# The second node stage of a three-layer graph network: the merge done head by head, with the bias inside it

## The reference

```
out = segment_sum(xl[src] * alpha, dst) + b1      # a softmax over the edges that end in a node, self loop included
h   = elu(out)                                    # what the second layer starts from
x   = layernorm(x + gatv2(h));  x = layernorm(x + gat(x))
```

## Time and profile before

| | us |
|---|---|
| median of 3 runs (4007.61 to 4011.79) | 4010.43 |
| profiled execution, its own time | 4004.83 |
| its span | 4003.0 |
| DVE busy in the span | 3296.9 (82%) |
| POOL busy in the span | 2765.2 (69%) |
| node stage 1: first L1360 to the MEMSET L1474 that opens edge stage 1 | 1319.49 to 1511.99 |

### The profile page before, as it was taken

One profiled execution on the slowest core, in us unless ns is written; L12 is line 12 of the kernel. 1 busy time (PEld: TensorE's weight loads), 2 busy tenths in 40 slices (PEclk: granted clock), 3 DMA queues, 4 the chain that ended last, 5 costly groups with the idle time before them and its releaser, 6 DMA issues. The chain is left out here.

```text
span 4003.0 us, 115501 instructions
## 1 busy us (share of the span) xinstructions
PE 3522.5 (88%) x30761; PEld 2584.0 (65%) x30762; DVE 3296.9 (82%) x10046; ACT 1278.9 (32%) x4356; POOL 2765.2 (69%) x3039
## 2 busy tenths in 40 slices
PE   6699999999999668999999999977678888787885
PEld 5577777777777456777777777745445555555543
DVE  6768888888888885888888888876688898888886
ACT  4433333333333463333333333324111111111113
POOL 5577777777776467777777777723777777777760
PEclk9899999999999899999999999989799999899989
DMA  4344444444443124444444444435455555555544
GB/s 99 116 131 136 136 131 136 136 135 132 134 136 106 58 70 135 136 135 131 136 136 135 131 136 136 131 96 186 134 143 140 143 145 143 141 144 138 144 109 129
DMA packets 279405, 520.84 MB, mean 130 GB/s; under 512 B 98391, under 2 KB 165121, under 8 KB 279313
## 3 DMA queue, kind: packets, MB, share of 16 engines
q0 software_dynamic: 120320, 338.39, 31.2%
q1 hardware_dynamic: 158993, 181.36, 15.1%
HBM read 484.05 MB, written 35.46 MB: 130 GB/s over the span
## 5 line engine op out<-in xcount | busy, mean ns | idle before, releaser
L704 POOL DMA_INDIRECT gathered<-table,idx x2496 | 2501.4, 1002 | 787.6 <-issue 526.0
L1120 PE MATMUL pS<-gathered,Dm 128*128 128x264 f32 x4992 | 1689.5, 422 | 107.7 <-DVE Dm L1533 58.9
L1520 DVE TENSOR_TENSOR acc_mem<-acc_mem,pS 128x264 f32 x2496 | 1043.6, 418 | 144.8 <-PE pS L1120 105.6
L1059 PE MATMUL pZ<-DT,x 128*128 128x128 bf16 x9984 | 1090.2, 221 | 14.1 <-DVE DT L1480 11.5
L1059 PEld LDWEIGHTS pZ<-DT,x 128*128 x9984 | 874.2, 98 | 325.0 <-issue 51.7
L873 ACT ACTIVATE reluT<-pZ 128x256 f32<-128x256 f32 x1664 | 637.1, 383 | 1128.5 <-PE pZ L1065 1098.6
L1120 PEld LDWEIGHTS pS<-gathered,Dm 128*128 128x128 f32 x4992 | 797.2, 200 | 239.5 <-DVE gathered L1551 104.9
L1065 PE MATMUL pZ<-ident,gathered 128*128 128x128 f32 x3328 | 934.6, 281 | 11.9 <-DMA gathered<-table,idx 11.8
L1551 DVE TENSOR_TENSOR gathered<-gathered 128x256 f32<-128x256 f32 x2496 | 941.6, 417 | 1.8 <-ACT gathered L865 1.0
L1533 DVE TENSOR_TENSOR Dm<-pS,rel_items 128x256 f32<-128x256 f32 x1239 | 513.8, 415 | 0.0
L1065 PEld LDWEIGHTS pZ<-ident,gathered 128*128 128x128 f32 x3328 | 470.4, 141 | 16.2 <-DMA gathered<-table,idx 14.3
(11 more groups left out here) (230 smaller groups left out, 3211.4 us busy)
## 6 DMA issues: line engine op xcount, KB each, us to landing
DT<-rel_dram SPq DMA_DIRECT2D x156, 512.0 KB
gathered<-table,idx POOLq DMA_INDIRECT x2496
table<-xls SPq DMA_DIRECT2D x147, 132.0 KB, 2.0
flags<-flag_dram SPq DMA_DIRECT2D x416, 32.0 KB
flags<-flag_dram SPq DMA_DIRECT2D x52, 256.0 KB
gathered<-table SPq DMA_DIRECT2D x98, 132.0 KB, 2.1
gathered<-in_x SPq DMA_DIRECT2D x98, 128.0 KB, 2.1
hx_dram<-gathered SPq DMA_DIRECT2D x49, 128.0 KB, 1.7
```

Of the source, the lines that this page charges most:

```text
L704: nc.gpsimd.indirect_dma_start(out=G[:, b, i, :], out_offset=None, in_=tab[l], in_offset=bass.IndirectOffsetOnAxis(ap=idx[:, b, i:i + 1], ...
L1059: mm = nc.tensor.matmul(z_slot(i)[:, half], x3[:, bass.ds(tk[i], 1), s, half].rearrange("p o c -> p (o c)"), moving, start=(s == 0), stop= ...
L1120: nc.tensor.matmul(pS[:, i % 4, 0:ROW], Dm[:, i % 8, :], G[:, at[0], at[1], :], start=True, stop=True).then_inc(seg_done, 1)
L1520: link(v.tensor_tensor(acc_at(n), acc_at(n), pS[:, n % 4, 0:ROW], ALU.add))
```

## The change

`merged` does not multiply by repeated numbers any more. It runs over the four heads and for each does one `scalar_tensor_tensor` on 64 columns, own * wx + bias, with wx as a scalar for each partition; then, behind a semaphore of its own, four more, sum * wn + own. The addition L1363 and POOL's `biased` are gone, with `o_ready`; ACT's exponential waits for `acc_read`. The wait for the weights that POOL had moves to DVE's first merge. The branches for other layers that `merged` held (it is called for l = 1 alone) are taken out.

```
 def biased(t, b, h):                                                    # gone, on POOL
-    pool.wait_ge(acc_read, t + 1)
-    nc.gpsimd.tensor_tensor(tmp[:, b, :], tmp[:, b, :], bias[:], ALU.add).then_inc(o_ready, 1)
-tiles(pool, (biased, 0), (clear, 0), (self_sum, 4))
+tiles(pool, (clear, 0), (self_sum, 4))
 def exponent(t, b, h):                                                  # ACT
-    act.wait_ge(o_ready, t + 1)
+    act.wait_ge(acc_read, t + 1)
 def merged(t, b, h):                                                    # DVE
-    v.tensor_tensor(hv(own[:, b, 0:D]), hv(own[:, b, 0:D]), of_tile(wx, t), ALU.mult)
-    v.tensor_tensor(hv(to), hv(num), of_tile(wn, t), ALU.mult).then_inc(node_step, 1)
-    dve.wait_ge(node_step, t + ((l - 1) * TILES + 1))
-    v.tensor_tensor(to, to, own[:, b, 0:D], ALU.add).then_inc(acc_read, 1)
+    if static(t) and t == 0:
+        dve.wait_ge(w_in, W_IN[1])
+    C = D // H
+    for k in range(H):
+        of = slice(k * C, (k + 1) * C)
+        ins = v.scalar_tensor_tensor(mine[:, of], mine[:, of], wx[:, bass.ds(t, 1), k], bias[:, of], ALU.mult, ALU.add)
+    ins.then_inc(node_step, 1)
+    dve.wait_ge(node_step, t + 1)
+    for k in range(H):
+        of = slice(k * C, (k + 1) * C)
+        ins = v.scalar_tensor_tensor(to[:, of], num[:, of], wn[:, bass.ds(t, 1), k], mine[:, of], ALU.mult, ALU.add)
+    ins.then_inc(acc_read, 1)
```

More of the change, by code:

```diff
@@ L247, in gnn_program @@
         elu_step = sem("elu_step")
-        o_ready = sem("o_ready")
         self_step = sem("self_step")
@@ L653, in later_low @@
                         low(t, b, h)
-                def biased(t, b, h):
-                    pool.wait_ge(acc_read, t + 1)
-                    nc.gpsimd.tensor_tensor(tmp[:, b, :], tmp[:, b, :], bias[:], ALU.add).then_inc(o_ready, 1)
                 def self_sum(t, b, h):
@@ L664, in self_sum @@
                     nc.gpsimd.tensor_tensor(zs[:, b, :], xls[:, b, 0:D], xr[:, b, :], ALU.add).then_inc(self_z, 1)
-                if l == 1:
-                    pool.wait_ge(w_in, W_IN[1])
                 if l == 2:
@@ L1350, in merged @@
                     num = acc[:, bass.ds(t, 1), 0:D].rearrange("p o r -> p (o r)")
[L1351 to L1354, removed]
+                    to, mine = tmp[:, b, :], own[:, b, 0:D]
+                    if not (static(t) and t < 2):
                         dve.wait_ge(h_ready, t - 1)
[L1356 to L1359, removed]
-                    v.tensor_tensor(hv(own[:, b, 0:D]), hv(own[:, b, 0:D]), of_tile(wx, t), ALU.mult)
-                    v.tensor_tensor(hv(to), hv(num), of_tile(wn, t), ALU.mult).then_inc(node_step, 1)
-                    dve.wait_ge(node_step, t + ((l - 1) * TILES + 1))
-                    v.tensor_tensor(to, to, own[:, b, 0:D], ALU.add).then_inc(acc_read, 1)
-                    if l == 1:
-                        if static(t) and t == 2:
-                            scale_attention(1)
+                    dve.wait_ge(own_in[b], (h + 1) * 16)
+                    if static(t) and t == 0:
[10 more added lines that the diff above has]
+                    ins.then_inc(acc_read, 1)
+                    if static(t) and t == 2:
+                        scale_attention(1)
                 def stats(t, b, h):
```

## The result

The changed kernel takes 4059.17 us in the median of four runs (4053.2 to 4061.8), against 4009.02 (4007.19 to 4011.79) for the kernel before on the same chip: a ratio of 1.0122, with a 95% interval of 1.0109 to 1.0134. It is slower by 50 us. The profiled execution took 4059.56, with a span of 4057.7; the one of before 4004.83.

A forecast was written before the change was run, and what follows sets the result against it. DVE was taken to bound the stage at 3.77 us a tile, PE's ring close behind at 3.61. Terms 28 - 20 + 33 + 1 - 2 = +40 gave 4050 on the median; own range 4040 to 4062, wider range 4012 to 4062.

The forecast's parts named there:

- Each operation: Each of the eight 64-column DVE merge operations: 0.20 us start to start, lasting about 0.28.
- The merge in the loop: DVE's eight operations plus one semaphore: 1.71 us against 1.14 before, +0.57 a tile, +28 us for 49 tiles.
- My upper bound of 0.23 for each of the eight: Merge with the sequencer's register work in line: 0.23 each, 1.95 in all, +0.81 a tile, +40 us.
- What goes with POOL's addition: DVE's L1395 no longer waits for POOL's addition L657: 0.42 for 48 tiles, -20 us.
- what is late next: POOL's earlier L630 and L664 meet DVE's L1395 and L1400: 0.75 in 44 steps, +33 us, and +1 us.
- The race: Behind the merge, POOL's L630 starts ahead of DVE's L1395 by 10 to 40 ns.
- The rival "its own form": L1395's double time is its form, not POOL; each of the eight costs 0.067 more: +52, 4062; chance 6%.
- The tail: Stage's end: PE waits for the last h with slower DVE, so the tail shortens by up to 1.8: -2 us.
- the reversed: DVE's L1395 comes ahead of POOL's L630, leaving a 0.17 loss in 44 steps: +13, 4024; chance 16%.
- the split race: POOL and DVE each come first in one of the loop's two tiles: +26, 4037; chance 18%.
- the -22 us: How the forecast sum would move if the eight started 0.14 apart instead of 0.20.

The follow-up runs named there:

- the three writes: Changed kernel with three write-only memsets (344, 128 and 128 columns) on POOL ahead of the clearing, in this stage alone: 4025.84 against 4010.69, ratio 1.0038.
- the small gap: Changed kernel with one write of 128 columns on POOL ahead of the clearing: 4032.2 against 4008.82, ratio 1.0055.
- the self-loop sum first: Changed kernel with POOL's self-loop sum put ahead of the clearing behind the merge: 4045.84 against 4010.69, ratio 1.0089.

## Why the prediction was right

The forecast was 4050 and slower; it came at 4059. The mechanism was right in both halves, and in their signs. Two terms of the sum were mis-sized.

The start of L1388 (old L1393) in each of the 49 tiles, after less before and counted from the first merge, divides the 48.2 us of the stage: 0.5 for the first tile, 0.9 over the next six, 44.8 over the 40 tiles of the loop that follow (1.12 each, the same at every pair of tiles), 0.4 for the last two, and 1.7 for what follows.

- **Each operation: right.** Lasting 0.28 and 0.20 apart, as forecast. Outside the loop the whole merge is what I had built from the rows of before, 1.71:

```profile
1546.24 0.87 DVE L1353 SCALAR_TENSOR_TENSOR gathered<-gathered,bias 128x64 f32<-128x64 f32 x4
1547.15 0.87 DVE L1358 SCALAR_TENSOR_TENSOR gathered<-acc_mem,gathered 128x64 f32<-128x64 f32 x4
1547.94 0.28 DVE L1388 TENSOR_SCALAR gathered<-gathered 128x256 f32<-128x256 f32 x1
```

  From 1546.24 to 1547.94 it is 1.70. A constant scalar gave 0.137 for my estimate of 0.14, and a load of 0.06 for my 0.055 to 0.07.

- **The merge in the loop: mis-sized.** The step that failed is "I take 0.20, because ... the sequencer of L1361 works while L1360 still runs", with its one wait at 0.11. In the loop, the merge takes 1.84. The last of the first four to the first of the second is 1.06 - 0.60 = 0.46 us, against 0.91 - 0.60 = 0.31 in the rows just above. The sequencer's row for this line shows what stands in the difference:

```profile
L1358 DVEq FUSED_REGOPS  x160: 93/96/110, 1352.0 to 1543.0; - x160
```

  There are four of them a tile, one for each head. Three run beside the operation ahead. The first can't: the wait for `node_step` stands ahead of it, so its 0.1 begins only when the first group is through. The run with constant scalars bears this out: there the work is 0.057, and the same distance is 0.36 in the loop for 0.25 outside it, so 0.11 in place of 0.15; with fixed addresses, and no such work, it is 0.32 at both places. In both runs with such work the loss is 0.05 more than the row, and what that is no row shows. Before, the wait belonged to L1363, whose address depends on nothing (the earlier trace rows is of L1361, which waited for nothing and was covered). The other part is at the loop's turn, 0.60 of "issue" for 0.36 in the earlier trace rows. From the start of L1401 to the next L1353 it is 0.77 there, where the old L1406 to L1360 took 0.63: 0.14 for two tiles. That makes 1.84 - 1.71 + 0.07 = 0.20 a tile; the run with fixed addresses puts it at 0.24, and the step itself shows 1.12 for the forecast 0.90. In 40 tiles: 0.22 x 40 = 9 us. My upper bound of 0.23 for each of the eight had the right cause in the wrong place: it covers this case (1.95 for 1.84), but it would have put the cost on all eight.

- **What goes with POOL's addition, and what is late next: right.** Forecast -0.42 and +0.75, net +0.33 a tile. From the run without the addition alone: 4.10 - 3.77 = 0.33. The race fell to POOL, by 0.03 us where 0.01 to 0.04 was forecast, in 42 tiles for my 44. The Trainium skill ("SBUF — State Buffer", section "Who interferes with whom") says that a DVE instruction with two SBUF inputs and a GpSimd instruction that reads SBUF exclude each other, and that the first to issue decides who waits. The runs agree, with 0.65 and 0.95 where POOL is first, 0.43 and then 0.62 or 0.95 where DVE is (0.95 behind the longer of POOL's reads), and with 0.42 where POOL only writes or where one input comes from PSUM.

- **The rival "its own form": refuted.** The Trainium skill ("Vector Engine (DVE) Microarchitecture Reference", "Points that are easy to get wrong") has this form, with two SBUF sources that are not bf16, at half throughput. Three runs (the three writes, the small gap, the self-loop sum first) show it at 0.42 to 0.43 for 256 columns where POOL doesn't read ahead of it, with both sources in SBUF, and the run with constant scalars at 0.219 for 64.

- **The tail: wrong in sign.** Forecast -2, measured +1.7. I had PE turn the last h as soon as it was there. It came 3.49 us after the end of L1390 (1551.05) instead of 1.84. From that transpose to the MEMSET it is 6.86 us in both kernels. PE before the end, after the change:

```profile
1546.06 1.15 PE L980 MATMUL pS<-W,gathered 128*128 128x260 f32 x4
1547.04 1.03 PE L984 MATMUL pS<-W,gathered 128*128 128x256 f32 x4
...
1550.90 2.10 PE L980 MATMUL pS<-W,gathered 128*128 128x260 f32 x4
1552.79 1.80 PE L984 MATMUL pS<-W,gathered 128*128 128x256 f32 x4
1554.43 0.27 PE L995 MATMUL pS<-x,gathered 128*128 128x256 bf16 x1
1554.54 0.38 PE L967 MATMUL pZ<-ident,gathered 128*128 128x128 f32 x2
```

  The eight matmuls of L980 and L984 took 2.01 us from the first's start to the last's end at 1546, and 3.69 at 1550.9, where the granted clock is 0.51, the lower of its two levels. The 1.68 between them is the tail's excess over before (3.49 - 1.84 = 1.65) to 0.03. The other 2 us of the error are not the clock's: L980 had begun at 1550.90, 0.15 before the last h was there, so the transpose stood behind these products in PE's order. It had been the same before the change (products from 1503.17, h at 1503.29), so the 1.84 that I wanted back was the time of these products, and a slower DVE did not shorten it.

  As to the clock: in the loop PE had waited for h 19 times, up to 1.3 us, which it hadn't before the change (it waited for ACT before as well), and before the change the clock was 1.00. That the idling caused the lower clock is what the profiles suggest (from 1400 to 1450 it was 1.00 in the runs with steps up to 4.13, and 0.81 to 0.93 in those with 4.24 and more) and no run here sets it alone. That a low stretch fell on the last products is chance as far as is known.

The sum again, with these sizes: 40, + 9 for the merge in the loop, + 3.7 for the tail, and - 4 for the nine tiles outside the loop, which lost 1.8 us together where my flat price for each tile came to some 6, because DVE isn't the bound in the first of them. That gives 48.7, for 48.2 measured; the last of these terms hid some of the first two. The chances were well placed: the reversed and the split race were near, since 0.15 us on POOL were enough to turn it. That it fell the forecast way, by 0.03 us, was in part luck. One slip in the text: the -22 us given there for operations 0.14 apart belongs to 0.145; for 0.14 it is -24.

## What to carry to other kernels

Shortening or removing an operation on an engine off the critical path moves all that stands behind it on that engine; ask what it will now run beside, to a few tens of ns, before counting the gain. Splitting one wide DVE operation into one for each head costs a fixed part each (0.07 us here) and, with a scalar for each partition, 0.06 more: at 64 columns that is twice the 0.067 of the columns themselves. A semaphore wait belongs on an instruction whose address is fixed, or the address work comes behind the wait; here the addresses cost 0.24 us a tile, the waits and the loop's turn together.

## What was not expected of the hardware

- Work that only writes, put on POOL ahead of its reads, made the changed kernel faster by 27 us (0.15 us of writing a tile) and 33 us (0.6 us a tile).
- How long a lock is held is less than the duration in the profile. The clearing, 0.40 long, held a DVE operation that came 0.03 later for 0.23; an operation of 0.72 that had waited held the next for 0.53.
- PE's granted clock fell from 1.00 to 0.81 in a stage where only DVE had become slower, and one low stretch fell on the one place where it can be seen to cost time, 1.68 us.
